# Two maxima over partitions in the setup of a cross-attention and feed-forward kernel: GpSimd's partition_all_reduce replaced by TensorE turns, row maxima and products with ones

## The reference

```python
x = x + xattn(layernorm(x), ctx, ctx, mask, ...)   # x: (16, 512, 256); ctx: (16, 64, 256)
x = x + ffn(layernorm(x), w1, b1, w2, b2)          # hidden width 1024
...
def xattn(query, key, value, mask, ...):           # one head of width 16
    qh = (query @ Wq) @ wq_h + bq_h;  kh = (key @ Wk) @ wk_h + bk_h;  vh = (value @ Wv) @ wv_h + bv_h
    attn = softmax(where(mask, -1e9, qh @ kh.T / sqrt(16)))
    return tile(attn @ vh, 16) @ Wo
def ffn(x, w1, b1, w2, b2):                        # each weight is (mean of its row's |w|) * sign(w)
    h = gelu(x @ bin(w1).T + b1);  return h @ bin(w2).T + b2
```

## Time and profile before

| | before |
|---|---|
| median of 3 runs | 413.41 us (412.19 to 414.05) |
| the profiled execution | 413.81 us, of which the span in the trace is 412.0 us |
| PE busy | 340.5 us (83%) |
| DVE busy | 331.0 us (80%) |
| POOL busy | 310.3 us (75%) |
| ACT busy | 259.2 us (63%) |
| first `first_product` starts | 70.38 us |

### The profile page before, as it was taken

How to read it: one execution, slowest core, us unless ns; L and a number is a source line. 1 busy time by engine, 2 the same in 40 slices (tenths; PEclk the granted TensorE clock), 3 DMA queues, 4 the chain that set the end, 5 groups by cost and what they waited for, 6 DMA issues and landing times. The chain is left out here.

```text
span 412.0 us, 7933 instructions
## 1 busy us (share of the span) xinstructions
PE 340.5 (83%) x2381; PEld 229.7 (56%) x2381; DVE 331.0 (80%) x718; ACT 259.2 (63%) x486; POOL 310.3 (75%) x462
## 2 busy tenths in 40 slices
PE   5987553999979889797979888888897979799794
PEld 4534341575847465665656565656474747475662
DVE  2857462999998979797989898989898979888655
ACT  1049313687868677676776767676776758586570
POOL 1310306687898989989898988888899898986866
PEclk9965555899999999999999999999999999999998
DMA  8700100101020201111111111010202020101012
GB/s 258 272 0 1 52 1 0 52 1 52 2 100 4 86 19 56 46 51 51 51 51 51 51 51 51 28 74 0 102 0 102 0 102 0 51 0 51 2 53 102
DMA packets 9424, 21.39 MB, mean 52 GB/s; under 512 B 1720, under 2 KB 4928, under 8 KB 9408
## 3 DMA queue, kind: packets, MB, share of 16 engines
q1 hardware_dynamic: 8496, 21.14, 14.2%
q10 hardware_dynamic: 912, 0.05, 0.1%
HBM read 12.80 MB, written 8.39 MB: 51 GB/s over the span
## 5 line engine op out<-in xcount | busy, mean ns | idle before, releaser
L650 DVE SCALAR_TENSOR_TENSOR h_lo<-h_sb,h_scale,h_hi 128x512 f16<-128x512 f32 x128 | 114.0, 921 | 12.5 <-POOL h_hi L415 9.5
L1188 PE MATMUL psZ<-sgn2T,h_hi 128*128 128x256 f16 x512 | 116.2, 273 | 0.5 <-DVE sgn2T L854 0.2
L1188 PE MATMUL psZ<-sgn2T,h_lo 128*128 128x256 f16 x512 | 116.0, 273 | 0.0
L1174 PE MATMUL psY<-x_hi,sgn1T 128*128 128x512 f16 x256 | 98.1, 383 | 1.6 <-ACT sgn1T L622 1.6
L499 ACT ACTIVATE h_sb<-psY,b_col,alpha1x 128x512 f32<-128x512 f32 x128 | 94.5, 776 | 6.5 <-PE psY L1174 3.9
L1174 PE MATMUL psY<-x_lo,sgn1T 128*128 128x512 f16 x256 | 98.2, 383 | 0.0
L1124 PE MATMUL psW<-ident,xh 128*128 128x128 f32 x256 | 36.5, 288 | 47.5 <-POOL xh L400 47.5
L400 POOL TENSOR_SCALAR xh<-x,rstd,nmr 128x256 f32<-128x256 f32 x64 | 62.7, 989 | 3.4 <-issue 1.9
L1124 PEld LDWEIGHTS psW<-ident,xh 128*128 128x128 f32 x256 | 29.2, 146 | 59.4 <-POOL xh L400 56.9
L415 POOL TENSOR_SCALAR h_hi<-h_sb,h_scale 128x512 f16<-128x512 f32 x64 | 46.3, 726 | 20.4 <-PE psZ L1188 18.0
L1188 PEld LDWEIGHTS psZ<-sgn2T,h_hi 128*128 128x128 f16 x512 | 49.9, 97 | 13.7 <-DVE h_lo L650 4.6
(11 more groups left out here) (141 smaller groups left out, 538.3 us busy)
## 6 DMA issues: line engine op xcount, KB each, us to landing
x_in<-in_x SPq DMA_DIRECT2D x16, 512.0 KB, 3.2
out_x<-z_sb SPq DMA_DIRECT2D x15, 512.0 KB, 2.6
w_sb<-in_L_ffn_w SPq DMA_DIRECT2D x2, 1024.0 KB, 10.0
ctx_sb<-in_ctx SPq DMA_DIRECT2D x1, 1024.0 KB, 8.0
out_x<-z_sb SPq DMA_DIRECT2D x2, 256.0 KB, 2.2
wk_sb<-in_L_xattn_Wk SPq DMA_DIRECT2D x1, 256.0 KB, 3.0
wq_sb<-in_L_xattn_Wq SPq DMA_DIRECT2D x1, 256.0 KB, 3.3
wv_sb<-in_L_xattn_Wv SPq DMA_DIRECT2D x1, 256.0 KB, 8.1
```

The costliest lines, as they stand in the source:

```text
L650: nc.vector.scalar_tensor_tensor(out=h_lo[c % 4][:, :], in0=h_sb[c % 4][:, :], scalar=h_scale[:, :], in1=h_hi[c % 4][:, :], op0=ALU.mult, ...
L1174: last = nc.tensor.matmul(psY[c % 4][:, :], sgn1T[:, k, c * P:(c + 1) * P], part[slot][:, k, :], start=(n == 0), stop=(n == 2 * KD - 1))
L1188: last = nc.tensor.matmul(psZ[j // 2][:, (j % 2) * D:(j % 2 + 1) * D], part[c % 4][:, j * P:(j + 1) * P], sgn2T[:, c, :], start=(c == 0 an ...
```

## The change

The maximum over partitions is made in four steps instead of one. PE turns the column (or the four columns) so that the 128 partitions lie in one row each; DVE takes the maximum of each row; for the four columns DVE puts the four maxima on a 4x4 diagonal; PE multiplies a block of ones with it, which puts the maxima on all 128 partitions in PSUM; DVE reads them from there. The turned rows and the spread maxima lie in the banks `psZ1` (mags) and `psZ0` (top), so some later writers of these banks wait for the readers. POOL keeps no part of it. `hidden_scales` moves on DVE from the end of `body` -1 to right behind the statistics of x1.

```diff
@@ gpsimd
-            def top_of_hidden():
-                pool.wait_ge(top_ready, 1)
-                nc.gpsimd.partition_all_reduce(top_all[:, :], top[:, :], P,
-                                               bass.bass_isa.ReduceOp.max).then_inc(top_reduced, 1)
...
             norm(0, 0, 0, x_in[0])
-            pool.wait_ge(mags_ready, 4)
-            nc.gpsimd.partition_all_reduce(mags_all[:, :], mags[:, :], P,
-                                           bass.bass_isa.ReduceOp.max).then_inc(mags_reduced, 1)
-            pool.wait_ge(mags_reduced, 1)
             norm(0, 1, 0, x_in[1])
-            top_of_hidden()
             pool.wait_ge(loaded["b2"], 16)
@@ vector
+            dve.wait_ge(pe_mags, 1)
+            nc.vector.tensor_reduce(mags_top[:, :], psZ[1][0:4, 0:P], AX.X, ALU.max) \
+                .then_inc(mags_top_ready, 1)
+            dve.wait_ge(mags_top_ready, 1)
+            nc.vector.tensor_scalar(mags_diag[:, :], ident[0:4, 0:4], mags_top[:, :], None,
+                                    ALU.mult).then_inc(mags_diag_ready, 1)
             copy_keys(1)
-            dve.wait_ge(mags_reduced, 1)
+            dve.wait_ge(mags_spread, 1)
+            nc.vector.tensor_copy(mags_all[:, :], psZ[1][:, P:P + 4]).then_inc(mags_all_copied, 1)
+            dve.wait_ge(mags_all_copied, 1)
             nc.vector.tensor_tensor(mv_bound[:, :], mags_all[:, 0:2], mags_all[:, 2:4], ALU.mult) \
...
+            def largest_of_tops():
+                dve.wait_ge(pe_top, 1)
+                nc.vector.tensor_reduce(top_one[:, :], psZ[0][0:1, 0:P], AX.X, ALU.max) \
+                    .then_inc(top_one_ready, 1)
+            def take_top():
+                dve.wait_ge(top_spread, 1)
+                nc.vector.tensor_scalar(top[:, :], psZ[0][:, P:P + 1], LEAST_BOUND, None, ALU.max) \
+                    .then_inc(top_taken, 1)
...
                     raw_bn(1, x1).then_inc(raw_stats[1], 1)
+                    if is_body(i, par, -1):
+                        largest_of_tops()
                     bn(i, par + 1, 1)
+                    if is_body(i, par, -1):
+                        take_top()
+                        hidden_scales()
...
                     copy_V(3)
-                    hidden_scales()
@@ tensor
+            def turn_mags():
+                pe.wait_ge(mags_ready, 4)
+                nc.tensor.transpose(psZ[1][0:4, 0:P], mags[:, :], ident[:, :]).then_inc(pe_mags, 1)
+            def spread_mags():
+                pe.wait_ge(mags_diag_ready, 1)
+                nc.tensor.matmul(psZ[1][:, P:P + 4], ones[0:4, :], mags_diag[:, :],
+                                 start=True, stop=True).then_inc(mags_spread, 1)
+            def turn_top():
+                pe.wait_ge(top_ready, 1)
+                pe.wait_ge(M_copied, 4)
+                nc.tensor.transpose(psZ[0][0:1, 0:P], top[:, :], ident[:, :]).then_inc(pe_top, 1)
+            def spread_top():
+                pe.wait_ge(top_one_ready, 1)
+                nc.tensor.matmul(psZ[0][:, P:P + 1], ones[0:1, :], top_one[:, :],
+                                 start=True, stop=True).then_inc(top_spread, 1)
             def score_weights(n):
                 pe.wait_ge(khT_copied, n + 1)
+                if n == 1:
+                    pe.wait_ge(mags_all_copied, 1)
                 for k in range(KD):
+                    if n == 0 and k == 1:
+                        spread_mags()
...
                     attend(i, par + 1)
+                if is_body(i, par, -1):
+                    turn_top()
...
                     values(2)
+                    spread_top()
...
             turn_x(0, 0, 0)
+            turn_mags()
             score_weights(0)
```

More of the change, by code:

```diff
@@ L126, in xattn_ffn_kernel @@
         top = sb("top", [P, 1])
-        top_all = sb("top_all", [P, 1])
+        top_one = sb("top_one", [1, 1])
         pow2 = sb("pow2", [P, 1])
@@ L135, in xattn_ffn_kernel @@
         mags = sb("mags", [P, 4])
+        mags_top = sb("mags_top", [4, 1])
+        mags_diag = sb("mags_diag", [4, 4])
         mags_all = sb("mags_all", [P, 4])
@@ L188, in xattn_ffn_kernel @@
         mags_ready = sem("mags_ready")
-        mags_reduced = sem("mags_reduced")
+        pe_mags = sem("pe_mags")
+        mags_top_ready = sem("mags_top_ready")
+        mags_diag_ready = sem("mags_diag_ready")
+        mags_spread = sem("mags_spread")
+        mags_all_copied = sem("mags_all_copied")
         mv_steps = sem("mv_steps")
@@ L224, in xattn_ffn_kernel @@
         top_ready = sem("top_ready")
-        top_reduced = sem("top_reduced")
+        pe_top = sem("pe_top")
+        top_one_ready = sem("top_one_ready")
+        top_spread = sem("top_spread")
+        top_taken = sem("top_taken")
         scale_steps = sem("scale_steps")
@@ L827, in _ @@
             first_norm(0, 1)
+            def largest_of_tops():
[6 more added lines that the diff above has]
+                    .then_inc(top_taken, 1)
             def hidden_scales():
[L831 to L834, removed]
+                dve.wait_ge(top_taken, 1)
                 nc.vector.tensor_scalar(pow2[:, :].bitcast(U32), top[:, :].bitcast(U32), 0x7F800000,
                                         None, ALU.bitwise_and).then_inc(scale_steps, 1)
-                dve.wait_ge(scale_steps, 4)
+                dve.wait_ge(scale_steps, 3)
                 nc.vector.reciprocal(inv_pow2[:, :], pow2[:, :]).then_inc(scale_steps, 1)
@@ L840, in hidden_scales @@
                                         ALU.mult).then_inc(scale_steps, 1)
-                dve.wait_ge(scale_steps, 6)
+                dve.wait_ge(scale_steps, 5)
                 nc.vector.tensor_scalar(h_scale[:, :], inv_pow2[:, :], H_TOP, None,
@@ L1080, in turn_signs_1 @@
                 pe.wait_ge(M_copied, 4)
+                pe.wait_ge(top_taken, 1)
                 for k in range(KD):
```

## The result

The changed kernel took 397.89 us (median of 4 runs, 396.15 to 397.98), the kernel before 413.73 us in the runs beside it: a ratio of 0.9589, interval 0.9562 to 0.9617. (The two medians, divided, give 0.9617; the ratio on record is the lower one, and a later set of runs, experiment 5, has 0.9587 by the record and 0.9579 by the medians.) Of the 413.41 us of before, 0.9589 is 396.4 us.

A forecast was written before the change was run, and what follows sets the result against it. POOL's code changes around its two reductions bound the setup; the turn of x1 coming 14.3 us earlier gives 413.81 - 14.3 = 399.5 us for the profiled execution, 399.2 us as median; range 397.0 to 402.0.

The forecast's parts named there:

- What bounds it: Setup: POOL changes code to each reduction and back, some 5.7 and 7.1 us each; from 49.4 to 70.4 us everything follows POOL.
- Rival 3: POOL's idle times don't come from the reductions; only 0.77 us of work goes, 413 us; chance 0.03.
- rival 4: Slower: clock stays at 0.50 through the first bodies, each growing by up to 15 us; chance 0.02.
- First maximum, the small steps: Five steps replacing the reduction of `mags`, between 1.0 and 3.0 us: scales at 25.5 instead of 28.8, 3.3 us earlier.
- First maximum, what comes through: Of the earlier scales only 1.0 us reaches x1 of batch 0 (bounds 0.3 and 1.3), PE's products for M running on.
- Second maximum: Round for `top`: PE idles 1 us for `top_one`; turn of batch 1 starts at 44.9 instead of 49.41, 4.5 us earlier.
- Turn of x1: After 7.5 us of unbroken work PE, not POOL, sets it: start at 52.4 instead of 66.76, 14.3 us earlier.
- Rival 1: New waits lose more: POOL's `norm` of x1 becomes the gate or `spread_top` is dearer; 401.2 to 404 us; chance 0.09.
- The clock behind it: PE's clock rises 4.5 us after the first feed-forward product starts, at about 60.6 us; 1 us either way.
- rival 2: Clock rises before the first product, saving up to 3 us of half-speed work: 396 to 397.8 us; chance 0.08.

The follow-up runs named there:

- experiment 5: Changed kernel and kernel before, both unmodified, run once more: 397.16 us (ratio 0.9587) and 413.78 us (one run).
- experiment 1: Changed kernel plus two POOL reductions at the old places, results read by nobody: 411.79 us, ratio to the kernel before 0.9928.
- after: The changed kernel as first measured and profiled, against the kernel before: median 397.89 us, ratio 0.9589; profiled execution 397.82 us.
- after_again: The changed kernel run unmodified a second time, for another profile: 397.16 us, ratio to the kernel before 0.9587.
- spread_later: Changed kernel with the second maximum's spread behind batch 1's turn, its reading behind w1's signs, hidden_scales back at body -1's end: 400.33 us, ratio 0.9618.
- before_again: The kernel before, run unmodified again for a second profile: 413.78 us in its one run.
- experiment 4: Changed kernel with the second maximum's round moved later, measured twice: 400.33 us, ratio 0.9618, then 397.64 us, ratio 0.9584.
- second_only: Kernel before with only the second maximum (`top`) made on TensorE, the first still POOL's reduction: 405.39 us, ratio 0.9773.

## Why the prediction was right in what bounds the kernel and wrong in what comes through of the first maximum

**What bounds it: right.** POOL's idle times came with the reductions and went with them; experiment 1 puts them back without any other part of the old way. The nameless instructions between the two kinds of work mark the places. Rival 3 (not the reductions) and rival 4 (slower) are out. Section 4.1 (Engine selection) of the Trainium skill's GPSIMD Engine Reference, which sends a reduction along the partitions to GpSimd, did not hold here: the reduction is cheap at 0.39 us, the idle times around it are not, and the kernel without it takes 0.9589 of the time.

**First maximum, the small steps: right.** The scales were forecast 3.3 us earlier; complete `mags` to first copy of M went from 6.60 to 3.30. The row reduction took 0.28 (forecast 0.3), PE's product 0.28 (0.4).

**First maximum, what comes through: this step failed.** It said that little comes through because PE's products for M run until 30.7 "whatever the scales do", and took 1.0 us with an upper bound of 1.3. It was 2.8 us in `after` and 3.1 in `after_again` (x1 of batch 0 at 17.56 and 17.24 instead of 20.38, from T0). The 30.7 was read from one execution in which the clock fell 1.9 us behind T0, so that nearly all of these products ran at half clock; in the second profile of the same kernel they ended at 27.14. With POOL's late maximum that moment changed nothing in the time, so one profile could not show that it varies. In ten of the twelve profiles the fall comes at 4.0 to 5.2 us; at 4.9 or later PE is done in time and ACT's chain of 7.88 us is the path, which starts 3.4 us earlier, and at 4.0 (`after`) some 0.3 us of it is lost. `spread_later` is the case that I had worked out: with the fall at 1.8, its first score came at 9.69, where I had 31.3 - 21.73 = 9.57, and x1 gained 0.7. No run sets the clock by itself, so this rests on the rows of the profiles and not on an edit.

With the term at 2.8 the sum is 413.81 - 16.1 = 397.7 for the profiled execution, which measured 397.82. That it fits so closely is in part luck: T0 was 0.9 us earlier in that profile, and 1.0 us came back behind the first product. From `before_again` to `after_again` the way from T0 to the first product fell by 16.85 us (49.03 to 32.18), 2.5 more than forecast, of which 2.3 is this term.

Two slips in the sum change nothing of this: 399.5 less 0.4 is 399.1 and not 399.2, and the range's own terms end at 400.9 and not 401.2.

**Second maximum: right.** From x1 to the turn of batch 1 3.8 us were forecast (41.1 to 44.9) and 3.84 measured, and PE's wait for `top_one` of 1 us was 0.84. Moved away (experiment 4), the stretch is 1.1 us shorter, POOL becomes the gate, and the kernel isn't faster.

**Turn of x1: right.** PE and not POOL sets it; 7.5 us were forecast from the turn of batch 1, 7.56 measured. POOL's `xh` ended at 48.48, 1.3 us before PE was there (forecast 51.4 at worst against 52.4). Rival 1 is out.

**The clock behind it: another step that one profile misled.** The forecast had one rise, at 60.6 us. In `after` the clock rose at 52.1, before the first product, as rival 2 had it, was back at 0.50 from 55.6 to 58.9 us, and then rose to stay. The kernel before does the like in its second profile: up at 57.0, right behind turns and scores like those behind which it stayed at 0.50 in the first, down at 60.4, up again at 74.0. It cost nothing visible: the stretches from the first product to the end (342.65 and 340.79 us in the two profiles of the changed kernel, 341.62 and 341.77 in those of before) show no gain or loss beyond their own spread. Over all twelve profiles they go from 340.7 to 344.4 us, and what moves them was not followed. So the 396.4 us lie in the window of rival 2 (396 to 397.8), but not by its mechanism.

## What to carry to other kernels

A GpSimd instruction of another kind of code is not priced by its own row but by the idle time ahead of it and ahead of the next ordinary one: here 0.39 us of reduction cost 13 us of POOL, and for `mags` a turn, a row maximum, a 4x4 diagonal, a product and a copy replaced it in 2.2 us (21.16 to 23.37). When a late event is taken off a path, look at what else arrives there and whether its time was read at a clock that could have been another; a second profile of the kernel before shows what varies under the cover of the wait. Where a milestone follows the clock, compare distances between milestones over several profiles before crediting an edit.

## What the runs showed that I had not expected

- PE's clock fell at 1.8 to 5.2 us behind the same turn in the twelve profiles, though all but one of the kernels are alike up to there, and in two of them it had fallen once before (at 17.1 and 17.2 us) and risen at 20.5 and 20.6.
- Instructions of DVE and POOL that ran at the same time were long on either side: the masking took 2.48 us beside POOL's additions instead of 0.45 (`second_only`), and POOL's four `xh` took 4.20 us beside DVE's signs instead of 2.17 (`after`). That each is long because of the other is the reading; no run took one of them away.
